# Scratch rows in (b, d) order: gathered embedding rows stored straight from the gather's tile

## The chip, the cores and the metric

The kernel runs on one core of one Trainium2 chip. The metric is the device time of one execution in microseconds (us). Before the change it is 2498.87 us, the median of three runs (2496.68 to 2500.59). All data are float32 unless said otherwise.

## What is computed

A recommendation tower. For each of B = 2048 samples, 39 ids pick one row of 16 floats from each of 39 tables; this is x0, of shape (B, 39, 16). Three layers of a compressed interaction network follow, then a small dense network on the sums and 16 dense features.

```python
e = stack([tbl_f[ids[:, f]] for f in range(39)], axis=1)      # (2048, 39, 16)
x0 = xk = e; direct = []
for idx, (W, b) in enumerate([(w0, b0), (w1, b1), (w2, b2)]): # W: (39, 39 or 64, 128)
    z = relu(einsum('bhd,bkd,hks->bsd', x0, xk, W) + b[None, :, None])
    if idx != 2: xk = z[:, :64]; direct.append(z[:, 64:])
    else: direct.append(z)
h = concatenate([sum(concatenate(direct, 1), -1), dense_ctx], 1)
h = relu(h @ W_top1 + b_top1); h = relu(h @ W_top2 + b_top2)
y = h @ W_top3
```

Every layer is a matmul over the products x0[h] * xk[k], with the pair (h, k) as the contracted index and (b, d) as the columns.

## The kernel before, in words

Samples are worked on in GROUPS = 16 groups of P = 128, and each group in CHUNKS = 4 chunks of CB = 32 samples, N = 32 x 16 = 512 columns. The order of the columns in a chunk is free as long as all tiles agree; before, it is (d, b).

GpSimd gathers: for each of the F = 39 fields an indirect DMA (L409) brings 128 rows of 64 B into `emb`, with the sample as the partition, 39 x 16 floats in each. The products need the field as the partition. So TensorE (PE) transposes `emb` in eight pieces of 78 columns into PSUM (`transpose_group`, L760 to L769; the two tiles of `turned` lie over `hi_copy`), ScalarE (ACT) copies them into `stage` (`fill_stage`, L588), and SP stores `stage` in a scratch tensor in HBM, `x0_transposed` (`xt`), 39 rows plus WRAP = 20 repeated ones, each COLS = 32768 floats long (`store_group`, L292). From there SP and ACT load, for every chunk, `x0_diag` (three bands of 39 partitions, seven tiles, for layer 0; `diag_band`, L254) and `x0_pairs` (64 partitions twice, 19 tiles, each row broadcast to 64 partitions, for layers 1 and 2; `pairs_half`, L262, and the last row to all 128, L331). `x0_pairs` has two buffers, `x0_diag` has one.

VectorE (DVE) multiplies into `prod`, a ring of four slots of four tiles (L479). Most tiles go to PE as float32 (L775, `plain_part`). For some, the product is split in a high part, made by ACT (L610), and a low part, made by DVE or GpSimd (L251, `low_part`), and PE multiplies three times (L796, `split_part`). In layer 2 all low parts are GpSimd's. PE takes the split tiles of layer 2 one slot behind the plain ones (`BEHIND`).

Every engine has a hand-written order, a loop over groups with four chunks in its body. In iteration c of group bt:

- PE: layer 1 of the chunk, layer 0 of the next chunk, layer 2 of the chunk. At c = 1, slot 1 of layer 2, it transposes group bt + 1 after it has waited for `gathered`.
- DVE: the products in the same order, the sums over d of z2 and of `direct01` (L530, L520).
- ACT: its half of the next chunk's pairs, the splits, the hand-ons of z, at c = 1 `fill_stage(bt + 1)`, its band of the chunk after next (L259 to L260).
- GpSimd: the low parts of layer 1 (`lows_of(1)`), ten gathers (`GATHERS_AT`: fields 20 to 29 and 30 to 38 of group bt + 1 at c = 0 and 1, fields 0 to 9 and 10 to 19 of group bt + 2 at c = 2 and 3), the low parts of layer 2 (`lows_of(2)`). At the end of c = 1 it waits for `gathered` and loads the next indices (L397). At c = 2, ahead of the gathers, `start_group` waits for the indices and for `turned_ready`, so that `emb` may be overwritten.
- SP: two bands of the next chunk once `summed2` allows it; at c = 2 then `store_group(bt + 1)`; then, once `prod_ready` shows the other buffer free, its pairs half. At c = 3 the chunk loaded is the first of group bt + 1, after a wait for `xt_stored`.

In the start, the same steps run one after the other: gather, transpose, copy, store, load bands, load pairs.

Of the kernel before, what the change touches and what calls it, by code (L numbers as in the profile page):

```python
# [29 lines left out]
ALU = mybir.AluOpType  # L30
# [7 lines left out]
CHUNKS = 4  # L38
CB = P // CHUNKS
# [54 lines left out]
PLAIN_TILES = {n: [t for t in range(TX - 1 if n else T0) if t not in SPLIT_TILES[n]] for n in SPLITS}  # L94
W_ORDER = (1, 2, 0)
W_SPLITS = {n: len(SPLIT_TILES[n]) + (n > 0) for n in SPLITS}
X0_DIAG_DMAS, X0_PAIRS_DMAS, ST_DMAS = 2 * DIAG, 3, 4
RAW_DMAS, WEIGHT_DMAS, TOP_DMAS = 2, 3, 10
H1, H2, DENSE = 512, 256, 16
DENSE_ROWS = 2 * 32 + DENSE  # L100
# [26 lines left out]
def build(nc, tables, ids, dense_t, w0f, w0s, w1, w2, small, wt1, wt1c, wt2, out):  # L127
# [5 lines left out]
    with ctx:  # L133
# [17 lines left out]
        logit2 = sb("logit2", [P, NB])  # L151
        idx = sb("idx", [P, F], I32)
        emb = sb("emb", [P, F * D])
        stage = sb("stage", [P, CHUNKS, D // 2, CB])
        ident = sb("ident", [P, P])
        w_plain = [sb(f"w{n}_plain", [P, len(PLAIN_TILES[n]), S]) for n in SPLITS]

        w_hi = [sb(f"w{n}_hi", [P, W_SPLITS[n], S], F32R) for n in SPLITS]
# [28 lines left out]


        hi_copy = ctx.enter_context(nc.psum_tensor("hi_copy", [P, 2, N], F32))
        turned = [hi_copy[:, 0, :], hi_copy[:, 1, :]]  # L190


        direct01 = ps("direct01")
# [10 lines left out]
        w_split = sem("w_split")  # L204
        weights_in = sem("weights_in")
        top_weights_in = sem("top_weights_in")
        ident_zero = sem("ident_zero")
        ident_ready = sem("ident_ready")
        first_idx_in = sem("first_idx_in")
        idx_in = sem("idx_in")  # L210
        waits_held = sem("waits_held")
        gathered = sem("gathered")
        turned_ready = sem("turned_ready")
        stage_ready = sem("stage_ready")
        xt_stored = sem("xt_stored")
        x0_diag_in = sem("x0_diag_in")
        x0_pairs_in = [sem(f"x0_pairs_in{i}") for i in range(2)]
# [54 lines left out]
        def _(sp):  # L272
# [19 lines left out]
            def store_group(bt):  # L292

                first = ahead(bt * (P * D))
                sp.wait_ge(stage_ready, 2 * (bt + 1))
                cols = xt[:, bass.ds(first, P * D)].rearrange(
                    "f (c e n) -> f c e n", c=CHUNKS, e=2)
                for half in range(2):
                    src = stage[half:2 * F:2].rearrange("p c d b -> p c (d b)")
                    sp.dma_start(cols[0:F, :, half, :], src).then_inc(xt_stored, 16)  # L300
                    sp.dma_start(cols[F:F + WRAP, :, half, :], src[0:WRAP]).then_inc(xt_stored, 16)

            def load_chunk(bt, c, store=False):

# [81 lines left out]

        @block.gpsimd
        def _(pool):
            nc.gpsimd.memset(ident[:], 0.0).then_inc(ident_zero, 1)
            pool.wait_ge(ident_zero, 1)  # L390
            nc.gpsimd.affine_select(out=ident[:], in_=ident[:], compare_op=ALU.not_equal, fill=1.0,
                                    base=0, pattern=[[-1, P]], channel_multiplier=1
                                    ).then_inc(ident_ready, 1)

            def load_indices(bt):

                pool.dma_start(idx[:], ids[bass.ds(bt * P, P), :]).then_inc(idx_in, 16)  # L397
# [1 line left out]
            def start_group(bt, first):  # L399
                if first:  # L400
                    pool.wait_ge(first_idx_in, 16)
                else:
                    pool.wait_ge(idx_in, 16 * bt)
                    pool.wait_ge(turned_ready, 2 * bt)
                    pool.sem_inc(waits_held, 1)

            def gather(fields):
# [50 lines left out]
        def _(dve):  # L458
# [56 lines left out]
            def sum01(bt, c):  # L515

                dve.wait_ge(direct01_ready, 2 * (bt * CHUNKS + c) + 2)
                if c == 0:
                    dve.wait_ge(window01_stored, 16 * (bt + 1))
                nc.vector.tensor_reduce(window01[:, c * CB:(c + 1) * CB],  # L520
                                        direct01[:].rearrange("p (d b) -> p b d", b=CB),
                                        AXIS.X, ALU.add).then_inc(summed01, 1)

            def sum2(bt, c):

                dve.wait_ge(direct2_ready, bt * CHUNKS + c + 1)
                if c == 1:
                    dve.wait_ge(window2_stored, 16 * (bt + 1))
                at = (c + CHUNKS - 1) % CHUNKS * CB
                nc.vector.tensor_reduce(window2[:, at:at + CB],  # L530
                                        z[2][:].rearrange("p (d b) -> p b d", b=CB),
                                        AXIS.X, ALU.add).then_inc(summed2, 1)

            dve.wait_ge(xk0_ready, 1)
# [50 lines left out]

        @block.scalar
        def _(act):
            def fill_stage(bt):  # L588
                if not (isinstance(bt, int) and bt == 0):
                    act.wait_ge(xt_stored, 16 * ST_DMAS * bt)  # L590
                for q in range(2):
                    act.wait_ge(turned_ready, 2 * bt + q + 1)
                    nc.scalar.copy(stage[0:2 * F, :, 4 * q:4 * q + 4, :].rearrange("p c d b -> p d c b"),
                                   turned[q][0:2 * F, :].rearrange("p (d c b) -> p d c b", d=4, c=CHUNKS)
                                   ).then_inc(stage_ready, 1)

            assert lows(2, V) <= 1

            def round_splits(n, some, slot, pos, used_by, chunk):
# [71 lines left out]
                nc.scalar.copy(w_hi[n][0:w_raw[n].shape[0]].rearrange("p t s -> p (t s)"), w_raw[n]  # L671
                               ).then_inc(w_hi_ready, 1)
            act.wait_ge(weights_in, 16 * WEIGHT_DMAS)
            fill_stage(0)
            act.wait_ge(xt_stored, 16 * ST_DMAS)
            act.wait_ge(w0_summed, 2)
            act.wait_ge(w_split, 3)
# [11 lines left out]
            def group(bt, last):  # L689
# [4 lines left out]
                for c in range(CHUNKS):  # L694
                    chunk = bt * CHUNKS + c
                    slot, pos = SL0 + chunk * SLC, SL0 + c * SLC
                    act.wait_ge(prod_ready, slot + 1)
                    if c < CHUNKS - 1:
                        load_second_half(bt, c + 1)
                    elif not last:  # L700
                        load_second_half(bt + 1, 0)
                    round_splits(1, slice(0, EARLY[1]), slot, pos, used_by, chunk)
                    direct_2(chunk, slot)
                    if not (last and c == CHUNKS - 1):
                        copy_xk0(chunk + 1)
                    round_splits(1, slice(EARLY[1], None), slot, pos, used_by, chunk)
                    slot, pos = slot + SLX, pos + SLX
                    if not (last and c == CHUNKS - 1):
                        round_splits(0, slice(0, None), slot, pos, used_by, chunk)

                        act.wait_ge(prod_ready, slot + SL0)
                    hand_on(1, xk2, b1_sb, slot)
                    nc.scalar.activation(direct01[0:HALF], z[1][HALF:P], ACT.Relu, bias=b1_sb[HALF:P]
                                         ).then_inc(direct01_ready, 1)
                    if c + 2 < CHUNKS:
                        load_last_band(bt, c + 2)
                    elif not last:
                        load_last_band(bt + 1, c + 2 - CHUNKS)
                    if last and c == CHUNKS - 1:
                        round_splits(2, slice(0, None), slot, pos, used_by, chunk)  # L720
                    else:
                        slot, pos = slot + SL0, pos + SL0
                        round_splits(2, slice(0, EARLY[2]), slot, pos, used_by, chunk)
                        hand_on(0, xk1, b0_sb, slot)
                        act.wait_ge(summed01, chunk + 2)
                        direct_0()
                        if c == 1 and not last:
                            fill_stage(bt + 1)

                            act.wait_ge(stage_ready, 2 * (bt + 2))  # L730
                        round_splits(2, slice(EARLY[2], None), slot, pos, used_by, chunk)

            with act.Fori(0, GROUPS - 1) as bt:
# [23 lines left out]

        @block.tensor
        def _(pe):
            def transpose_group(bt):  # L760
                pe.wait_ge(gathered, 16 * F * (bt + 1))
                if not (isinstance(bt, int) and bt == 0):
                    pe.wait_ge(stage_ready, 2 * bt)
                for d in range(D // 2):

                    ins = nc.tensor.transpose(turned[d // 4][0:2 * F, d % 4 * P:(d % 4 + 1) * P],  # L766
                                              emb[:, d:F * D:D // 2], ident[:])
                    if d % 4 == 3:
                        ins.then_inc(turned_ready, 1)  # L769

            def plain_part(n, t, i, held, first, last):

                rows = P if n else R0_LAST if t + i == T0 - 1 else R0
# [32 lines left out]
                        lows[s[3]] = lows[s[3]] + 1  # L806
                ins.then_inc(slot_free, 1)

            def layer(n, slot, pos, lows, turn=None, turn_at=None):

                last_slot = len(FIRST_TILE) - 1
                for k, t in enumerate(FIRST_TILE):
# [3 lines left out]
                    pe.wait_ge(prod_ready, slot + k + 1)  # L816
                    for i in plain:
                        plain_part(n, t, i, held, k == 0 and i == plain[0], False)
                    if k == turn_at:
                        transpose_group(turn)  # L820
                    if not BEHIND[n]:
                        split_parts(n, k, lows)
                    elif k > 0:
# [16 lines left out]
                    lows[s[3]] = lows[s[3]] + 1  # L840
                ins.then_inc(slot_free, SL0)

            pe.wait_ge(ident_ready, 1)
            transpose_group(0)
            pe.wait_ge(w0_summed, 2)
            pe.wait_ge(w_split, 3)
            pe.wait_ge(weights_in, 16 * WEIGHT_DMAS)
# [2 lines left out]
            def group(bt, last):  # L850
                for c in range(CHUNKS):
# [8 lines left out]
                        layer0(slot, pos, lows)  # L860
                        slot, pos = slot + SL0, pos + SL0
                    pe.wait_ge(summed2, chunk + 2)
                    if c == 1 and not last:
                        layer(2, slot, pos, lows, bt + 1, 1)
                    else:
                        layer(2, slot, pos, lows)

            with pe.Fori(0, GROUPS - 1) as bt:
                group(bt, False)
# [88 lines left out]
```

## Time and profile before

| | us |
|---|---|
| median of three runs | 2498.87 |
| the profiled execution | 2500.31 |
| its span | 2498.6 |
| PE busy | 2385.2 (95%) |
| VectorE busy | 2230.4 (89%) |
| GpSimd busy | 1709.7 (68%) |
| ScalarE busy | 1501.2 (60%) |
| bytes moved by DMA | 481.11 MB, mean 193 GB/s |

How to read it: the profile is one execution. Matmuls are pipelined and their ends are modelled, so a busy PE need not be at its peak. The granted clock is a share of full speed (1.00 is 2.4 GHz). DMA queue q1 is SP's, q10 is ScalarE's, q0 is GpSimd's. A DMA's packets on q1 and q10 are its contiguous rows, and one more on each engine for the count. "Idle before, releaser" tells how long an engine stood before an instruction and what ended that.

### The profile page before, as it was taken

The page shows a single profiled execution, that of the slowest core. Times are in us where ns is not written, and L with a number is a line of the kernel's source. Part 1 is how long each engine was busy: PE and PEld are TensorE (multiplying, and loading weights), DVE is VectorE, ACT ScalarE, POOL GpSimd, SP SyncE. Part 2 cuts the span into 40 slices and gives each one's busy share as a digit, 9 for nine tenths or more (in the row PEclk, how much of TensorE's full clock was granted, in tenths as well). Part 3 has the DMA queues.
Part 4 walks back from the last instruction along what each step waited for, and adds up shares of the span by engine and source line. Part 5 has one row for each costly group of instructions (what it writes and reads, how often), then busy time and mean ns, then how long its engine had stood idle before and what let it go on. Part 6 is the DMA issues. An engine that isn't in the chain of part 4 may idle for free.

```text
span 2498.6 us, 27181 instructions
## 1 busy us (share of the span) xinstructions
PE 2385.2 (95%) x7840; PEld 1468.9 (59%) x7840; DVE 2230.4 (89%) x1358; ACT 1501.2 (60%) x1798; POOL 1709.7 (68%) x1093
## 2 busy tenths in 40 slices
PE   0599999999999999999999999999999999999999
PEld 0266666666666666666666666666666666666653
DVE  0599999999999999999999999999999999999960
ACT  0366666666666666666666666666666666666652
POOL 6478777777777777677777777777776777754340
PEclk9899999999999999999999999999999999999999
DMA  2877877787777778777787877788787777867620
GB/s 69 237 207 190 222 210 199 190 214 209 190 210 209 208 182 217 208 197 199 213 216 178 215 211 202 190 215 218 181 211 212 206 182 213 222 183 202 199 62 0
DMA packets 267897, 481.11 MB, mean 193 GB/s; under 512 B 20075, under 2 KB 42715, under 8 KB 267797
## 3 DMA queue, kind: packets, MB, share of 16 engines
q1 hardware_dynamic: 146950, 275.14, 41.7%
q10 hardware_dynamic: 100480, 200.29, 28.9%
q0 software_dynamic: 20448, 5.45, 1.9%
q8 instruction: 9, 0.15, 0.0%
q14 instruction: 10, 0.08, 0.0%
HBM read 470.96 MB, written 9.84 MB: 192 GB/s over the span
## 4 chain that ended last, share of the span: by engine, by line
PE 70%; POOL 11%; issue 6%; DMA 6%; DVE 4%; ACT 2%; ACTq 0%; SPq 0%; POOLq 0%; DVEq 0%
PE z L796 34%; PE z L775 33%; POOL emb L409 7%; DMA emb<-in_tbl,idx 5%; DVE prod L479 4%; POOL lo_parts L251 4%; PE z L897 1%; DMA x_pairs<-x_transposed 1%; PE xk L897 1%; PE hi_copy L766 1%; ACT hi_parts L610 1%; PE direct L897 1%; DMA x_diag<-x_transposed 0%; ACT xk L630 0%; ACT xk L631 0%
## 5 line engine op out<-in xcount | busy, mean ns | idle before, releaser
L479 DVE TENSOR_TENSOR prod<-x_pairs,xk 128x2048 f32<-128x2048 f32 x640 | 1440.9, 2281 | 119.4 <-PE z L796 73.1
L775 PE MATMUL z<-prod,w_plain 128*128 128x512 f32 (+2 forms) x2688 | 1264.6, 595 | 40.2 <-DVE prod L479 40.2
L251 POOL TENSOR_TENSOR lo_parts<-prod,hi_parts 128x1024 fp32r<-128x1024 f32 x384 | 917.3, 2389 | 509.0 <-ACT hi_parts L610 486.0
L610 ACT CAST hi_parts<-prod 128x1024 fp32r<-128x1024 f32 x766 | 798.6, 1049 | 715.6 <-DVE prod L479 512.0
L796 PE MATMUL z<-hi_parts,w_lo 128*128 128x512 f32 (+1 forms) x1536 | 857.7, 558 | 1.1 <-DVE lo_parts L251 0.7
L409 POOL DMA_INDIRECT emb<-in_tbl,idx x624 | 701.9, 1125 | 196.0 <-issue 175.3
L775 PEld LDWEIGHTS z<-prod,w_plain 128*128 128x128 f32 (+2 forms) x2688 | 510.2, 190 | 440.1 <-issue 365.7
L796 PE MATMUL z<-hi_parts,w_hi 128*128 128x512 f32 (+1 forms) x1536 | 611.0, 398 | 0.0
L796 PE MATMUL z<-lo_parts,w_hi 128*128 128x512 f32 (+1 forms) x1536 | 606.7, 395 | 0.0
L796 PEld LDWEIGHTS z<-hi_parts,w_lo 128*128 128x128 f32 (+1 forms) x1536 | 289.9, 189 | 196.3 <-issue 145.0
L796 PEld LDWEIGHTS z<-lo_parts,w_hi 128*128 128x128 f32 (+1 forms) x1536 | 292.3, 190 | 189.5 <-issue 148.4
L796 PEld LDWEIGHTS z<-hi_parts,w_hi 128*128 128x128 f32 (+1 forms) x1536 | 288.5, 188 | 67.8
L251 DVE TENSOR_TENSOR lo_parts<-prod,hi_copy 128x1024 fp32r<-128x1024 f32 x256 | 310.2, 1212 | 2.9 <-ACT hi_copy L624 2.8
L479 DVE TENSOR_TENSOR prod<-x_diag,xk 117x2048 f32<-117x2048 f32 (+1 forms) x128 | 256.7, 2006 | 57.7 <-ACT xk L654 57.7
L624 ACT CAST hi_copy<-prod 128x1024 fp32r<-128x1024 f32 x256 | 259.1, 1012 | 2.1 <-DVE lo_parts L251 0.5
L630 ACT ACTIVATE xk<-z,columns 64x512 f32<-64x512 f32 x128 | 83.0, 648 | 145.3 <-PE z L796 143.7
L251 DVE TENSOR_TENSOR lo_parts<-prod,hi_parts 117x1024 fp32r<-117x1024 f32 x128 | 150.1, 1210 | 0.0
L245 POOL TENSOR_TENSOR half_parts<-prod,half_parts 64x512 fp32r<-64x512 f32 x64 | 81.9, 1280 | 5.5
L631 ACT ACTIVATE xk<-z,columns 64x512 f32<-64x512 f32 x128 | 83.5, 652 | 1.6
L766 PE MATMUL hi_copy<-ident,emb 128*78 128x128 f32 x128 | 18.3, 288 | 65.8 <-DMA emb<-in_tbl,idx 65.7
L606 ACT CAST half_parts<-prod 128x512 fp32r<-128x512 f32 x128 | 78.7, 615 | 0.0
L766 PEld LDWEIGHTS hi_copy<-ident,emb 128*78 128x78 f32 x128 | 14.3, 149 | 78.2 <-issue 78.1
(69 smaller groups left out, 652.0 us busy)
## 6 DMA issues: line engine op xcount, KB each, us to landing
x_pairs<-x_transposed SPq DMA_DIRECT2D x64, 2432.0 KB, 16.2
x_pairs<-x_transposed ACTq DMA_DIRECT2D x64, 2432.0 KB, 18.6
x_diag<-x_transposed SPq DMA_DIRECT2D x128, 546.0 KB
x_diag<-x_transposed ACTq DMA_DIRECT2D x64, 546.0 KB
x_pairs<-x_transposed SPq DMA_DIRECT2D x64, 256.0 KB, 19.6
emb<-in_tbl,idx POOLq DMA_INDIRECT x624
x_diag<-x_transposed SPq DMA_DIRECT2D x128, 78.0 KB
x_transposed<-stage SPq DMA_DIRECT2D x32, 156.0 KB
```

The lines of the kernel that those rows point to most:

```text
L245: engine.tensor_tensor(half_parts[0:HALF], held[0:HALF, at, :], hi, ALU.subtract).then_inc(done, 1)
L251: engine.tensor_tensor(lo_parts[0:rows, place:place + m, :], held[0:rows, at:at + m, :], hi, ALU.subtract).then_inc(done, 1)
L409: nc.gpsimd.indirect_dma_start(out=emb[:, f * D:(f + 1) * D], out_offset=None, in_=tables[f], in_offset=bass.IndirectOffsetOnAxis(ap=idx[: ...
L479: nc.vector.tensor_tensor(prod[0:rows, pos % RING, 0:n, :], a, xk.unsqueeze(1).broadcast_to([rows, n, N]), ALU.mult).then_inc(prod_ready, 1)
L606: nc.scalar.copy(half_parts[:], held[:, at, :]).then_inc(hi_ready, 1)
L610: nc.scalar.copy(hi_parts[0:rows, place:place + m, :], held[:, at:at + m, :]).then_inc(hi_ready, 1)
L624: nc.scalar.copy(hi_copy[:, 0:m, :].bitcast(F32R), held[:, at:at + m, :]).then_inc(hi_copied, 1)
L630: nc.scalar.activation(xk[0:HALF], z[layer][0:HALF], ACT.Relu, bias=b[0:HALF])
L631: nc.scalar.activation(xk[HALF:P], z[layer][0:HALF], ACT.Relu, bias=b[0:HALF]).then_inc(xk_ready[layer], 1)
L775: return nc.tensor.matmul(z[n][:], w, held[0:rows, i, :], start=first, stop=last)
L796: ins = nc.tensor.matmul(z[n][:], w, x, start=(first and i == 0), stop=(last and i == len(terms) - 1))
L897: ins = nc.tensor.matmul(acc[0:w.shape[1]], w, x, start=(k == 0), stop=(k == len(terms) - 1))
```

## The change

The scratch rows are laid out with the columns of a group in (b, d) order. SP waits for the gathers and stores `emb` as it is: for sample b and field f, 16 floats go to row f at column 16 b. Each group is stored by two DMAs in place of four. The transposes on PE, `turned`, `ident`, `stage`, ScalarE's two copies and the semaphores `turned_ready` and `stage_ready` are gone. GpSimd's `start_group` waits for `xt_stored`, since the store now reads `emb`. The two sums over d read (b, d) order. The loads of bands and pairs keep their shapes.

```diff
-X0_DIAG_DMAS, X0_PAIRS_DMAS, ST_DMAS = 2 * DIAG, 3, 4
+X0_DIAG_DMAS, X0_PAIRS_DMAS, ST_DMAS = 2 * DIAG, 3, 2
...
             def store_group(bt):
                 first = ahead(bt * (P * D))
-                sp.wait_ge(stage_ready, 2 * (bt + 1))
-                cols = xt[:, bass.ds(first, P * D)].rearrange(
-                    "f (c e n) -> f c e n", c=CHUNKS, e=2)
-                for half in range(2):
-                    src = stage[half:2 * F:2].rearrange("p c d b -> p c (d b)")
-                    sp.dma_start(cols[0:F, :, half, :], src).then_inc(xt_stored, 16)
-                    sp.dma_start(cols[F:F + WRAP, :, half, :], src[0:WRAP]).then_inc(xt_stored, 16)
+                sp.wait_ge(gathered, 16 * F * (bt + 1))
+                cols = xt[:, bass.ds(first, P * D)].rearrange("f (b d) -> b f d", d=D)
+                rows = emb[:].rearrange("p (f d) -> p f d", d=D)
+                sp.dma_start(cols[:, 0:F, :], rows).then_inc(xt_stored, 16)
+                sp.dma_start(cols[:, F:F + WRAP, :], rows[:, 0:WRAP, :]).then_inc(xt_stored, 16)
...
             def start_group(bt, first):
...
                     pool.wait_ge(idx_in, 16 * bt)
-                    pool.wait_ge(turned_ready, 2 * bt)
+                    pool.wait_ge(xt_stored, 16 * ST_DMAS * bt)
...
                 nc.vector.tensor_reduce(window01[:, c * CB:(c + 1) * CB],
-                                        direct01[:].rearrange("p (d b) -> p b d", b=CB),
+                                        direct01[:].rearrange("p (b d) -> p b d", d=D),
                                         AXIS.X, ALU.add).then_inc(summed01, 1)
...
-            def fill_stage(bt):
-                if not (isinstance(bt, int) and bt == 0):
-                    act.wait_ge(xt_stored, 16 * ST_DMAS * bt)
-                for q in range(2):
-                    act.wait_ge(turned_ready, 2 * bt + q + 1)
-                    nc.scalar.copy(stage[0:2 * F, :, 4 * q:4 * q + 4, :].rearrange("p c d b -> p d c b"),
-                                   turned[q][0:2 * F, :].rearrange("p (d c b) -> p d c b", d=4, c=CHUNKS)
-                                   ).then_inc(stage_ready, 1)
...
-                        if c == 1 and not last:
-                            fill_stage(bt + 1)
-
-                            act.wait_ge(stage_ready, 2 * (bt + 2))
...
-            def transpose_group(bt):
-                pe.wait_ge(gathered, 16 * F * (bt + 1))
-                if not (isinstance(bt, int) and bt == 0):
-                    pe.wait_ge(stage_ready, 2 * bt)
-                for d in range(D // 2):
-
-                    ins = nc.tensor.transpose(turned[d // 4][0:2 * F, d % 4 * P:(d % 4 + 1) * P],
-                                              emb[:, d:F * D:D // 2], ident[:])
-                    if d % 4 == 3:
-                        ins.then_inc(turned_ready, 1)
...
-                    if k == turn_at:
-                        transpose_group(turn)
```

## Rows read from the trace of the kernel before

**Rows 1.** The page: busy share of each engine, DMA by slice, queues.
```profile
PE 2385.2 (95%) x7840; PEld 1468.9 (59%) x7840; DVE 2230.4 (89%) x1358; ACT 1501.2 (60%) x1798; POOL 1709.7 (68%) x1093
...
DMA  2877877787777778777787877788787777867620
...
q10 hardware_dynamic: 100480, 200.29, 28.9%
```

**Rows 2.** Busy time by stretch: us, engines (instructions), granted clock, DMA share, GB/s.
```profile
1000.00:1153.00 153.00, 152.16 (x508) 95.00 (x507) 145.93 (x88) 98.09 (x118) 114.74 (x73) 1.00 0.77 199
1181.00:1189.00 8.00, 7.37 (x31) 5.22 (x32) 6.26 (x3) 6.22 (x9) 6.67 (x5) 1.00 0.28 73
1189.00:1197.00 8.00, 8.00 (x30) 5.18 (x29) 6.98 (x5) 5.28 (x6) 3.02 (x3) 1.00 0.93 208
1201.00:1205.00 4.00, 4.00 (x15) 2.46 (x13) 4.00 (x3) 3.02 (x5) 3.08 (x4) 1.00 1.07 337
```

**Rows 3.** GpSimd's index load in the loop: duration ns, first and last start us.
```profile
L397 POOL DMA_DIRECT2D idx<-in_ids x14: 577/580/587, 176.1 to 2061.5; - x14
```

**Rows 4.** ScalarE by time: start us, us, line, operation [idle before <-releaser].
```profile
1115.68 0.62 ACTq L265 DMA_DIRECT2D x_pairs<-x_transposed  x1
...
1151.46 0.63 ACTq L265 DMA_DIRECT2D x_pairs<-x_transposed  x1
...
1184.15 1.06 ACT L593 COPY stage<-hi_copy 78x512 f32<-78x512 f32 x2
...
1188.88 0.62 ACTq L265 DMA_DIRECT2D x_pairs<-x_transposed  x1
...
1210.93 0.33 ACTq L259 DMA_DIRECT2D x_diag<-x_transposed  x1
```

**Rows 5.** PE by time, layer 2 of chunks c = 1 and c = 2.
```profile
1181.63 1.09 PE L766 MATMUL hi_copy<-ident,emb 128*78 128x128 f32 x8 [1.06 <-DMA emb<-in_tbl,idx]
1182.47 0.48 PE L796 MATMUL z<-hi_parts,w_lo 128*128 128x512 f32 x1
...
1217.95 0.80 PE L796 MATMUL z<-hi_parts,w_lo 128*128 128x512 f32 x1
```

**Rows 6.** Packets of a queue at 30:50, 1.9:2.1 and 1107.8:1108 us; one issue.
```profile
DMA packets 512, 0.13 MB, mean 7 GB/s; under 512 B 256, under 2 KB 512, under 8 KB 512
q0 software_dynamic: 512, 0.13, 6.5%
...
q1 hardware_dynamic: 111, 0.02, 50.7%
...
q1 hardware_dynamic: 110, 0.05, 89.2%
...
1106.89 0.38 SPq L338 DMA_DIRECT2D sums<-logit  x1
sums<-logit SPq DMA_DIRECT2D x1, 64.0 KB, 2.1
```

**Rows 7.** SP's DMA issues by time, around the store of a group.
```profile
1173.03 0.32 SPq L259 DMA_DIRECT2D x_diag<-x_transposed  x1
...
1185.51 0.94 SPq L300 DMA_DIRECT2D x_transposed<-stage  x1
...
1189.72 0.70 SPq L265 DMA_DIRECT2D x_pairs<-x_transposed  x1
1190.60 3.81 SPq L331 DMA_DIRECT2D x_pairs<-x_transposed  x1
```

**Rows 8.** GpSimd by time: last gather of a group, next gathers, subtractions; the first subtraction.
```profile
1173.39 0.94 POOL L409 DMA_INDIRECT emb<-in_tbl,idx  x1 [0.30 <-issue]
...
1199.69 0.99 POOL L409 DMA_INDIRECT emb<-in_tbl,idx  x1 [0.44 <-issue]
...
1214.72 7.38 POOL L251 TENSOR_TENSOR lo_parts<-prod,hi_parts 128x1024 fp32r<-128x1024 f32 x3 [1.25 <-ACT hi_parts L610]
...
108.63 2.39 POOL L251 TENSOR_TENSOR lo_parts<-prod,hi_parts 128x1024 fp32r<-128x1024 f32 x1 [26.53 <-ACT hi_parts L610]
```

**Rows 9.** The chain that ended last, in the start: start us, us, what.
```profile
51.52 2.44 DMA emb<-in_tbl,idx
...
62.20 0.35 SPq L259
```

More of the change, by code:

```diff
@@ L153, in build @@
         emb = sb("emb", [P, F * D])
-        stage = sb("stage", [P, CHUNKS, D // 2, CB])
-        ident = sb("ident", [P, P])
         w_plain = [sb(f"w{n}_plain", [P, len(PLAIN_TILES[n]), S]) for n in SPLITS]
@@ L189, in build @@
         hi_copy = ctx.enter_context(nc.psum_tensor("hi_copy", [P, 2, N], F32))
-        turned = [hi_copy[:, 0, :], hi_copy[:, 1, :]]
         direct01 = ps("direct01")
@@ L206, in build @@
         top_weights_in = sem("top_weights_in")
-        ident_zero = sem("ident_zero")
-        ident_ready = sem("ident_ready")
         first_idx_in = sem("first_idx_in")
@@ L212, in build @@
         gathered = sem("gathered")
-        turned_ready = sem("turned_ready")
-        stage_ready = sem("stage_ready")
         xt_stored = sem("xt_stored")
@@ L388, in _ @@
         def _(pool):
[L389 to L393, printed above, removed]
             def load_indices(bt):
@@ L530, in sum2 @@
                 nc.vector.tensor_reduce(window2[:, at:at + CB],
-                                        z[2][:].rearrange("p (d b) -> p b d", b=CB),
+                                        z[2][:].rearrange("p (b d) -> p b d", d=D),
                                         AXIS.X, ALU.add).then_inc(summed2, 1)
@@ L673, in _ @@
             act.wait_ge(weights_in, 16 * WEIGHT_DMAS)
-            fill_stage(0)
             act.wait_ge(xt_stored, 16 * ST_DMAS)
@@ L807, in split_parts, with layer @@
                 ins.then_inc(slot_free, 1)
-            def layer(n, slot, pos, lows, turn=None, turn_at=None):
+            def layer(n, slot, pos, lows):
                 last_slot = len(FIRST_TILE) - 1
@@ L841, in layer0 @@
                 ins.then_inc(slot_free, SL0)
-            pe.wait_ge(ident_ready, 1)
-            transpose_group(0)
             pe.wait_ge(w0_summed, 2)
@@ L862, in group @@
                     pe.wait_ge(summed2, chunk + 2)
[L863 to L866, printed above, removed]
+                    layer(2, slot, pos, lows)
             with pe.Fori(0, GROUPS - 1) as bt:
```

## The prediction

> **What bounds the kernel now.** I read the busy shares first [rows 1]: TensorE (PE) is busy 95% of the span, VectorE 89%, GpSimd 68%, the 16 DMA engines 71 to 78% by slice. A share of 95% still hides a start without PE, so I looked at one stretch in the middle: of 153 us PE has 152.16 busy, at the full granted clock of 1.00 [rows 2]. In the steady part whatever stops PE moves the end one for one, and nothing gives it back. The period of a group (128 samples, four chunks) comes from the index load that GpSimd issues once a group: from 176.1 to 2061.5 us there are 13 periods, 145.03 us each [rows 3]. ScalarE's load of the second pairs half marks a fixed place in every chunk: 1115.68, 1151.46, 1188.88 [rows 4]. One ordinary chunk is 35.78 us, four of them 143.12, so a group has 1.91 us that three of its chunks do not have; the chunk that has them is c = 1, 37.42 us long. In PE's order of work it is visible: eight transposes begin at 1181.63 after 1.06 us of waiting for the last gathered rows, and the next split matmul stands at 1182.47, 0.84 us on [rows 5]. 1.06 + 0.84 = 1.90.
>
> **What goes.** The transposes and their wait: 15 in the loop (group 0's lie in the start), 15 x 1.91 = 28.6 us less, all of it on PE. ScalarE's two copies into `stage` (1.06 us at 1184.15 [rows 4]) lie beside PE's work and are worth nothing: ScalarE waits for products again right behind them. In the start they are on the path, counted below. The identity and its two instructions on GpSimd run before the indices have landed: nothing. The two sums on VectorE read PSUM with stride 1 instead of 32; at 0.68 us each with VectorE not setting the pace, I take nothing; if half of them fell away (128 x 0.34 us) PE would still set the pace.
>
> **What comes: the store.** Before, a group's 236 KB leave as runs of 1 KB: 4 DMAs, 39 x 4 x 2 + 20 x 4 x 2 = 472 rows. After, a run is one field of one sample, 16 floats = 64 B: 128 x 39 + 128 x 20 = 7552 rows, 472 on each of 16 engines where 30 were. The profile counts one packet for each row on SP's and ScalarE's queues, so I price the store by packet. No row shows 64 B written to HBM, so the price is bounded from both sides. From below: (a) GpSimd's gathers write 64 B rows packed eight to a packet: 6.5% of 16 engines in 20 us over 256 full packets is 81 ns a packet, 10 ns a row [rows 6]. (b) SP's load of the indices, 156 B rows: 111 packets in 0.2 us is 29 ns from packet to packet on an engine, of which 50.7%, 15 ns, busy [rows 6]. (c) SP's store of the sums, 512 B rows, 128 partitions, to HBM: 110 packets, 89.2% of 16 x 0.2 us, 26 ns each [rows 6]. (c) is the same queue, direction, memory and number of partitions, and (b) says that a row three times shorter isn't issued faster. I take 26 ns: 472 x 0.026 = 12.3 us a group. From above I take twice that, 52 ns (24.5 us), since a row far below 512 B might need its surroundings read before it is written.
> The page "DMA: Bandwidth & Descriptors" of the Trainium skill (Specifications) states that below 512 B the DMA engine does read-modify-write; no row of this trace shows such a write. By that rule the store would stand at the upper end, and the sum at the third rival's time.
>
> **Where the store lies.** Four DMAs at 0.8 to 0.9 us of SP's time become two. SP issues it behind the bands of the chunk (1173.0 to 1175.2) and ahead of the pairs (1189.72) [rows 7]. It waits now for `gathered`, whose last count comes at 1181.6 (that is what PE waited for [rows 5]): the last gather, begun at 1173.39 [rows 8], takes 8.2 us to land beside the bands against 2.44 us alone [rows 9]. First packet 0.9 us after the issue (sums store: issued 1106.89, packets from 1107.8 [rows 6]), so 1182.6. From 1187.0 (1188.88 less 1.9) ScalarE's half of the pairs asks for the same 16 engines, 64 x 19 rows of 2 KB, 76 per engine. A row of it costs 115 ns on average (28.9% of 16 x 2498.6 us over 100480 packets [rows 1]) and 147 ns in the stretch where both halves start (0.93 x 16 x 8 us over 208 GB/s x 8 us / 2048 B = 812 rows [rows 2]); 76 of them are 8.7 to 11.1 us, I take 10. If an engine takes one packet from each queue in turn, all 76 get in ahead of the store's end, since the store has 472. What bears this out is that gather, 5.8 us later in company. (The same page, Queues, rings and completion order, has the engines go round between queues by packets; the row agrees.) With 1.0 us from the last packet to the count (sums store: landed 2.1 us after the issue), the store has landed at 1182.6 + 12.3 + 10 + 1.0 = 1205.9.
>
> **Who waits for it.** `start_group` on GpSimd, at c = 2: before it waited for the transposes, long done; now the gathers of the group after next may not overwrite `emb` before the store has landed. Behind this wait are queued ten gathers (12.5 us with their gaps of 0.3) and then `lows_of(2)`, six subtractions that PE needs. Before: GpSimd reaches it at 1199.3, begins gathering at 1199.69, ends at 1213.5, idles 1.25 us, begins the first subtraction at 1214.72 [rows 8] and ends it at 1217.1; PE uses it at 1217.95 [rows 5]. Slack 1.25 + 0.85 = 2.1. In the new time, 1.9 earlier: 1199.3 + 2.1 - 1.9 = 1199.5 is the last moment without harm. So 1205.9 - 1199.5 = 6.4 us late; PE misses its low parts and stands. In general the loss is 0.472 t - 5.9 us for t ns per row. The loop has 14 such waits (the last two groups gather nothing; the one in the start is hidden, as the gathers for group 1 would end near 68 + 25 = 93 us and GpSimd's first subtraction, at 108.63, has 26.53 us of idle time ahead of it [rows 8]): 14 x 6.4 = 90 us.
> Others that wait: ScalarE's `load_last_band(bt+1, 0)` at 1210.93 [rows 4], 1209 in the new time, after 1205.9: nothing at 26 ns. SP's pairs stand behind the store in the same queue: 84 packets, some 12 us, landed near 1218, needed near 1224 + 6. Nothing, but this cover is gone at 40 ns, by when GpSimd's wait is longer anyway.
>
> **The start.** Gathers landed at 54.0, transposes, copies, four stores and landing, first band at 62.20 [rows 9]. After: 54.1 + 0.9 + 12.3 + 1.0 = 68.3, with no transposes to compete with: +6.1 us.
>
> **Sum.** -28.6 + 90 + 6.1 = +67.5 us on a span of 2498.6, 2566 us; the profiled execution took 2500.31, 1.7 more than its span, and 1.4 above the median 2498.87. So 2566 + 1.7 = 2568 us, 2.8% slower. This is the forecast, with 0.45.
>
> **Rivals.**
> First, the store hides (chance 0.22). If an engine overlaps a small packet of one queue with a large one of the other, or rows are packed as the gather's are, the 10 us drop out: landed at 1195.9, before 1199.5, loss zero up to t = 33 ns. For it: the 16 engines are only 28% busy from 1181 to 1189, and a share of 107% from 1201 to 1205 says that packets overlap [rows 2]. Against: late landings. Time: -28.6 + 6.1, 2478 us; with gather-priced rows (4.7 us) 2470. This is the other side from my forecast. It decides at a loss of 1.6 us per group, t = 16 with the full 10 us, or 37 without.
> Second, a partial hiding (0.05) between it and the forecast, about 1.5 us lost per group: 2499.
> Third, the short row costs double (0.23): 52 ns, loss 18.6 us x 14 = 261, start +18.4, -28.6: 2751 us. Then ScalarE also waits for it: landed at 1218, ScalarE at 1209, but it is the same delay and not added. For it: HBM writes of an eighth of the shortest write seen, 16 engines at once; each field's rows are 128 KB apart. Against: nothing but the steady 15 to 26 ns per short packet.
> Fourth, the edit moves the stall to ScalarE (0.05): if SP's 7552 rows block the unit that expands ScalarE's DMA too, ScalarE stands from 1187 until the store is nearly out, 1195; its next copy was due at 1188: 6 to 7 us for 15 groups, 90 to 105, about 2570. For it: SP's 3.81 us in one issue [rows 7].
> That the edit does nothing to PE isn't open: the transposes are gone from its queue.
>
> **Chances and range.** About 0.2% (5 us) is what a measurement here can tell from no change. Faster 0.23, same 0.05, slower 0.72. The range must take in the hidden case at its low end and the doubled price at its high end: 2465 to 2765. The likeliest case alone, t from 23 to 40 ns and 8.7 to 11.1 us of pairs, gives 2530 to 2670.
>
> **What would show it.** Right: a row "POOL emb <- DMA x_transposed<-emb" near 6 us x 14; PE idle before a split matmul of layer 2 at c = 2, waiting for GpSimd's low parts, nearly as large; chunk c = 1 down to 35.8 us, chunk c = 2 up to some 42; SP's queue with 113,000 more packets; the first band at 68 us. The first rival shows no such wait and 143.1 us a group. Wrong at the root: PE waiting for x_pairs or x_diag, which would say that DMA time as a whole, not the one wait, is the bound.

## The result and the profile after

The changed kernel takes 2468.41 us, median of four runs (2467.41 to 2470.75), against 2499.73 for the kernel before in the same runs: ratio 0.9876, 95% interval 0.9861 to 0.989. It is 31 us faster; I had forecast 2568 us, 68 us slower. What came is the first rival (2478 us, or 2470 with rows as cheap as the gather's): the store hides. One execution of the ten of an experiment below (the transposes back, with their wait) took 2771.23 us at a granted clock of 0.852 and stands in no comparison.

The page of the changed kernel: busy shares, DMA by slice, queues. They answer to [rows 1].

```profile
span 2465.7 us, 26690 instructions
...
PE 2366.6 (96%) x7712; PEld 1456.0 (59%) x7712; DVE 2229.2 (90%) x1358; ACT 1484.1 (60%) x1766; POOL 1706.1 (69%) x1091
...
DMA  2987878788787878878787887778778787877620
...
q1 hardware_dynamic: 260006, 275.13, 43.6%
```

SP's queue has 260006 packets, 113056 more than the 146950 before, as worked out (113280). The bytes are the same. All these rows cost the 16 engines 530 us of engine time together: 43.6% of 16 x 2465.7 less the 41.7% of 16 x 2498.6 of before. That would be 4.7 ns a row where I took 26; some of the difference of two large shares may be other rows' time, so the price is read from a clean stretch below.

One group in time. First GpSimd's index load, once a group (answers to [rows 3]); then ScalarE's issue of its pairs half in four chunks of one group and the next (answers to [rows 4]).

```profile
L382 POOL DMA_DIRECT2D idx<-in_ids x14: 574/579/582, 170.3 to 2031.9; - x14
```

```profile
1098.01 0.64 ACTq L258 DMA_DIRECT2D x_pairs<-x_transposed  x1
1133.79 0.63 ACTq L258 DMA_DIRECT2D x_pairs<-x_transposed  x1
1169.59 0.65 ACTq L258 DMA_DIRECT2D x_pairs<-x_transposed  x1
1205.39 0.63 ACTq L258 DMA_DIRECT2D x_pairs<-x_transposed  x1
1241.21 0.64 ACTq L258 DMA_DIRECT2D x_pairs<-x_transposed  x1
```

(2031.9 - 170.3) / 13 = 143.20 us a group, 1.83 less than 145.03. All chunks now have 35.8 us; the long one of 37.42 is gone. 15 x 1.83 = 27.5 us of the 31 to 33. The rest is in the start: VectorE's first product begins at 93.70 in place of 98.61, 4.9 us earlier.

The store by SP's issues, and GpSimd around its wait (answer to [rows 7] and [rows 8]).

```profile
1164.00 0.43 SPq L291 DMA_DIRECT2D x_transposed<-emb  x1
1164.71 3.15 SPq L292 DMA_DIRECT2D x_transposed<-emb  x1
1169.45 0.65 SPq L258 DMA_DIRECT2D x_pairs<-x_transposed  x1
```

```profile
1177.13 2.38 POOL L244 TENSOR_TENSOR lo_parts<-prod,hi_parts 128x1024 fp32r<-128x1024 f32 x1 [3.83 <-ACT hi_parts L586]
1180.08 0.98 POOL L394 DMA_INDIRECT emb<-in_tbl,idx  x1 [0.57 <-issue]
...
1194.90 7.38 POOL L244 TENSOR_TENSOR lo_parts<-prod,hi_parts 128x1024 fp32r<-128x1024 f32 x3 [1.19 <-ACT hi_parts L586]
```

Issued at 1164.0, 5.6 us ahead of ScalarE's pairs (I had 5.3), the store has its packets from 1165.0 to 1170.5 and has landed at 1171.7. SP's own pairs begin at 1170.5; ScalarE's first packet comes only at 1174.6, 5.0 us after its issue. GpSimd asks for the store at 1179.5. There is no wait: the 0.57 us before the gather at 1180.08 are issue. In the whole run GpSimd waits for the store once, 7.0 us, in the start, where nobody needs it.

SP's packets from 1166 to 1168 us (packets, MB, share of 16 engines):

```profile
DMA packets 2862, 0.18 MB, mean 92 GB/s; under 512 B 2862, under 2 KB 2862, under 8 KB 2862
...
q1 hardware_dynamic: 2862, 0.18, 89.3%
```

2862 rows in 2 us on 16 engines are 11.2 ns from row to row, 10 ns of it busy. 472 x 0.0112 = 5.3 us a group, not 12.3.

### The profile page after: what moved, and what is told of

Same layout as the page of the kernel before. It is cut to its first block, busy times and chain, and to the rows that moved or that the text cites. A ratio compares the mean times of both kernels' runs of the same rounds, so it can differ in the third digit from the quotient of the medians.

```text
span 2465.7 us, 26690 instructions
## 1 busy us (share of the span) xinstructions
PE 2366.6 (96%) x7712; PEld 1456.0 (59%) x7712; DVE 2229.2 (90%) x1358; ACT 1484.1 (60%) x1766; POOL 1706.1 (69%) x1091
## 3 DMA queue, kind: packets, MB, share of 16 engines
q1 hardware_dynamic: 260006, 275.13, 43.6%
## 4 chain that ended last, share of the span: by engine, by line
PE 95%; POOL 2%; DMA 2%; issue 1%; ACT 0%; DVE 0%; SPq 0%; ACTq 0%; POOLq 0%; DVEq 0%
PE z L735 46%; PE z L756 46%; POOL emb L394 1%; PE z L850 1%; PE xk L850 1%; DMA x_pairs<-x_transposed 1%; PE direct L850 1%; DMA x_diag<-x_transposed 0%; POOL lo_parts L244 0%; DVE prod L464 0%; DMA x_transposed<-emb 0%; ACT x_pairs L723 0%; DMA emb<-in_tbl,idx 0%; ACT hi_parts L586 0%; DMA idx<-in_ids 0%
## 5 line engine op out<-in xcount | busy, mean ns | idle before, releaser
L630 ACT COPY xk<-x_diag 117x512 f32<-117x512 f32 x64 | 37.3, 582 | 58.2 <-DMA x_diag<-x_transposed 58.2
L756 PE MATMUL z<-half_parts,w_lo 128*128 128x512 f32 x128 | 51.2, 400 | 0.0
```

Source lines behind the costliest of these rows:

```text
L756: ins = nc.tensor.matmul(z[n][:], w, x, start=(first and i == 0), stop=(last and i == len(terms) - 1))
```

## The experiments

The first four ran on one chip, the second four on another, on which the kernel before took 2511.29 us instead of 2498.9. Times of the second four are set against that one, and group periods against the unchanged loop of the last of them.

**The changed kernel again.**

> The changed kernel once more, beside the others of this call, as their measure. Theory (the gain is the eight transposes and their wait, 15 times, plus a shorter start): 2468 us, 1.83 us less per group than before (period of a group 143.2 us against 145.0), first product of VectorE near 94 us. What is open is the start: the first load of the pairs took 20.5 us in the changed kernel and 24.6 us before. If that belongs to the kernel it is 20 to 21 us again; if it is a matter of the single execution it differs.

2469.21 us (before: 2498.9; ratio 0.9882, 0.9865 to 0.9898). The first load of the pairs took 19.73 us from the issue on the chain that ended last, near the 20.5 of the first trace. Those are two executions of the changed kernel against one of the kernel before.

**The transposes back, with their wait.**

```diff
+                pe.wait_ge(gathered, 16 * F * (bt + 1))
+                for d in range(D // 2):
+                    ins = nc.tensor.transpose(hi_copy[0:2 * F, d // 4, d % 4 * P:(d % 4 + 1) * P],
+                                              emb[:, d:F * D:D // 2], ident[:])
+                ins.then_inc(turned_ready, 1)
```

> The changed kernel with the eight transposes of emb put back on PE at their old place, with the wait for the gathers, their result unused (no copies by ScalarE, the direct store stays). Theory (all of the loop's gain was PE's time): 15 x 1.9 us = 28 us more than the changed kernel, 2496 us, and a group's period of 145.0 us again. Rival (part of the gain came from ScalarE's copies, from stride-1 sums or from another order of the transfers): less than 20 us more, under 2488 us.

2496.84 us, 27.6 us above the changed kernel of the same call. The group has its old period, from GpSimd's index loads less the first:

```profile
L392 POOLq MOVE idx<-in_ids x14: 29/29/38, 167.0 to 2052.8; - x14
```

(2052.8 - 167.0) / 13 = 145.06. The chunks are 37.27, 36.33, 35.82 and 35.78 us by ScalarE's pairs. ScalarE's copies, the four stores in place of two, and the sums' stride of the kernel before are not put back here, so they were worth nothing that can be seen: the whole gain of the loop is PE's queue.

**The transposes back, without the wait.** The same, but they read a tile that nothing writes in the loop.

> As the one before, but the transposes read a tile that is never written in the loop, so PE doesn't wait for the gathers. Theory: only the transposes' own 0.84 us remain, 15 x 0.84 = 12.6 us more than the changed kernel, 2481 us. If the wait costs nothing by itself (PE would have stood there anyway): the same 2496 us as with the wait.

2474.24 us, only 5.0 above, not 12.6.

```profile
L394 POOLq MOVE idx<-in_ids x14: 29/29/38, 169.4 to 2035.7; - x14
```

143.56 us a group, 0.36 more. This does not mean that the transposes cost only 0.36 us. PE never stands in the middle of either kernel, and it runs at the full granted clock. First the changed kernel, then this one, from 400 to 2200 us (us, PE busy and its instructions, PEld, VectorE, ScalarE, GpSimd, granted clock, DMA share, GB/s):

```profile
400.00:2200.00 1800.00, 1800.00 (x5933) 1120.78 (x5932) 1743.89 (x1058) 1142.85 (x1356) 1336.04 (x845) 1.00 0.79 206
400.00:2200.00 1800.00, 1800.00 (x6022) 1125.38 (x6022) 1740.88 (x1056) 1142.47 (x1353) 1335.51 (x845) 1.00 0.79 206
```

Yet this one does more in the time. PE's block of eight plain matmuls, once a chunk, comes every 35.80 us in the changed kernel; here (start us, us, what; the transposes lie between the last two rows):

```profile
840.48 3.44 PE z L755 x8
876.14 3.44 PE z L755 x8
912.69 3.44 PE z L755 x8
```

35.66 us for a chunk without transposes, 36.55 for one with them. The transposes cost 0.89 us where they stand, 15 x 0.89 = 13.4 us, near the 12.6 expected. And every chunk, with or without them, is 0.14 us shorter than in the changed kernel, 64 x 0.14 = 9.0 us. Together that is 4.4 us more, 5.0 were measured. The shorter chunks are no time that PE took back from a wait, as there is none: its matmuls follow each other a little faster. In the kernel before, in the changed one and in the transposes with their wait a chunk is 35.80. This kernel has one more tile in SBUF (`fixed`, 2.5 KB a partition) than the kernel with the wait; whether that is the cause, no run here tells. So 2474.24 us can't be read as the price of the transposes, nor the 22.6 us up to 2496.84 as that of the wait. By PE's rows the kernel with both has, in the group at 1176 us, 1.01 us of waiting and 0.85 of transposes, together the 1.86 by which its group is longer.

**The first group stored in two parts.**

```diff
+            sp.wait_ge(first_gathered, 16 * WRAP)
+            sp.dma_start(cols[:, F:F + WRAP, :], rows[:, 0:WRAP, :]).then_inc(xt_stored, 16)
+            sp.dma_start(cols[:, 0:WRAP, :], rows[:, 0:WRAP, :]).then_inc(first_stored, 16)
+            sp.wait_ge(gathered, 16 * (F - WRAP))
+            sp.dma_start(cols[:, WRAP:F, :], rows[:, WRAP:F, :]).then_inc(xt_stored, 16)
```

> The changed kernel, with group 0 stored in two parts: fields 0 to 19 (with their repeated rows) as soon as they are gathered, fields 20 to 38 at the end. Everything else as in the changed kernel. Theory (rows cost near 11 ns each on an engine, 472 of them 5.5 us; now 152 stand behind the last gather, 1.8 us): the first band 3.5 us earlier, 2465 us. Rival (the landing is mostly fixed latency, or the pairs' load takes back what is gained): under 1.5 us, 2467 us or more.

2467.31 us (ratio to before 0.987, 0.9854 to 0.9887), 1.9 us less than the changed kernel beside it; their intervals overlap, so this isn't shown as a gain. Its chain in the start, and that of the changed kernel of the same call (start us, us, what):

```profile
54.30 3.34 DMA x_transposed<-emb
58.99 10.07 DMA x_diag<-x_transposed
69.86 23.70 DMA x_pairs<-x_transposed
93.77 2.30 DVE prod L476
```

```profile
54.92 6.64 DMA x_transposed<-emb
62.92 9.56 DMA x_diag<-x_transposed
73.27 19.73 DMA x_pairs<-x_transposed
93.22 2.30 DVE prod L464
```

The store lands in 3.34 us in place of 6.64, as expected, and the load of the pairs takes all of it back, 23.70 against 19.73. Both of my lines were half right: the price was, and so was the taking back.

**Store twice, store thrice.** The store itself made longer, at its place.

```diff
-                cols = xt[:, bass.ds(first, P * D)].rearrange("f (b d) -> b f d", d=D)
+                for to in (xt, *extra):
+                    cols = to[:, bass.ds(first, P * D)].rearrange("f (b d) -> b f d", d=D)
```

> The changed kernel with each group stored twice, the second time to a scratch tensor that nothing reads; all waits for the store wait for both. 944 rows of 64 B per engine, 11 ns each: 11 us, so now the store is still under way when ScalarE's half of the pairs starts. Theory A (an engine takes packets in turn, the store is held up by the 76 rows of 2 KB, 9 to 11 us): landed some 5 us after GpSimd's last harmless moment, 14 x 4 to 5 us, with 5.5 us in the start: near 2534 us. Theory B (small and large packets overlap, nothing is added): landed before GpSimd asks, 5.5 us in the start only: 2474 us.

> As the one before, with each group stored three times: 1416 rows per engine, 16.4 us. Theory A (in turn): landed near 10.7 us too late, 14 times, and 11 us in the start: 2630 us. Theory B (overlap): landed 0.7 us too late, 2489 us. In both GpSimd shows a wait for the store at c = 2; if the time rises without such a wait, the DMA time as a whole is the bound.

2610.89 us (ratio 1.04, 1.0382 to 1.0417) and 2680.08 us (1.0672, 1.0654 to 1.069). It is the mechanism of theory A, but its times were 2534 and 2630 us, too low by 77 and 50; 13 us of each are the slower chip. Twice, in the trace, GpSimd around the wait; and the packets of SP (q1) and ScalarE (q10) in 1090 to 1094, 1094 to 1098 and 1102 to 1106 us:

```profile
1099.11 2.36 POOL L246 TENSOR_TENSOR lo_parts<-prod,hi_parts 128x1024 fp32r<-128x1024 f32 x1 [3.85 <-ACT hi_parts L589]
1110.61 2.64 POOL L397 DMA_INDIRECT emb<-in_tbl,idx  x1 [9.14 <-DMA extra<-emb]
...
1126.90 0.80 PE L759 MATMUL z<-hi_parts,w_lo 128*128 128x512 f32 x1 [6.25 <-POOL lo_parts L246]
```

```profile
q1 hardware_dynamic: 5138, 0.33, 79.2%
q10 hardware_dynamic: 29, 0.06, 4.6%
...
q10 hardware_dynamic: 455, 0.93, 96.3%
q1 hardware_dynamic: 456, 0.03, 12.3%
...
q10 hardware_dynamic: 344, 0.67, 76.8%
q1 hardware_dynamic: 2078, 0.13, 42.9%
```

Alone, SP's rows pass at 5138 in 4 us. As soon as ScalarE's rows of 2 KB are there, the queues have 455 and 456: in turn, 140 ns for one of each, and the short rows crawl until the long ones are through. The counts keep together in stretches as short as 0.14 us, 10 to 23 of each and never more than 4 apart. The first issue was at 1086.11, GpSimd goes on at 1110.61: 24.5 us for 944 rows. GpSimd stands 9.14 us, PE 6.25 us for the low parts that are late. A group takes 152.74 us against 144.23 in the unchanged loop on that chip (the last kernel below), 8.5 more. All of it lies where PE stands, and standing is not all of it. PE has nothing to do from 1120.7 on; here is what was granted to it while it stood, and when it went on at 1126.90:

```profile
1123.00:1126.80 3.80, 0.00 (x0) 0.00 (x0) 0.00 (x0) 1.18 (x2) 3.48 (x3) 0.51 0.89 211
1126.90:1129.60 2.70, 2.70 (x6) 2.15 (x7) 0.00 (x0) 0.00 (x0) 2.60 (x2) 0.50 0.87 150
```

The granted clock fell to its lower level, 1.2 GHz, while PE stood, and PE's matmuls, which start 0.235 us apart otherwise, started 0.43 us apart until about 1129.7. From group to group this adds 1.6 to 3.0 us to the 6.3 to 6.4 us of standing, on average 2.3 (the third group and those after it). Three times: 157.1 us a group, 12.9 more, of which 10.4 are standing and the rest again the lower clock; GpSimd waits 225.6 us in all for the last copy. The waits of 0.8 to 1.1 us in the kernel before do not lower the clock; it is 1.00 from 400 to 2200 us.

**The store behind the pairs.**

```diff
-                if store:
-                    store_group(bt + 1)
...
                              ).then_inc(x0_pairs_in[c % 2], 16)
+                if store:
+                    store_group(bt + 1)
```

> The changed kernel with SP issuing the store of the next group behind its pairs of the chunk instead of ahead of them, nothing else. The rows wait in SP's queue for 84 large rows per engine. Theory (the place hides the store, and GpSimd's wait is on the path once it is late): landed near 25 us after the pairs' issue, 13 us too late, 14 times: near 2650 us. Rival (GpSimd's wait is taken up by its idle time, or ScalarE's wait comes first): under 2500 us, or more than 2650 with ScalarE named as the one that waits.

2685.81 us (ratio 1.0691, 1.0673 to 1.0709). Who waited for whom (us in total, times, longest):

```profile
POOL emb L394 <- DMA x_transposed<-emb: 236.8, 15, 17.7
...
PEld z L756 <- POOL lo_parts L244: 225.1, 133, 14.2
PE z L756 <- POOL lo_parts L244: 173.3, 31, 13.3
```

On its chip the changed kernel would take 0.988 x 2511.3 = 2481 us; a group takes 14.4 us more than the unchanged one there (158.66 against 144.23), and 14 x 14.4 = 202 us are the difference to within 3 us; I had expected 13 us of lateness. PE stands for 12.0 of the 14.4 us on average, and the other 2.4 go by the granted clock of 0.50 behind each stall. Nothing but the place in SP's order has changed, and the kernel goes from 1.2% faster to 6.9% slower. ScalarE, the other that waits for the store, is not named among the large waits.

**Rows by size, and two queues at once.** A tail behind the output: `probe_store(n)` stores 39 x 128 rows of n floats. ScalarE issues the load after the seventh store, and once more when it has landed, beside SP's last two stores.

```diff
+            for n in (16, 8, 16, 32, 64, 128, 256):
+                probe_store(n)
+                done += 1
+                sp.wait_ge(probe_stored, 16 * done)
+            sp.wait_ge(probe_loaded, 16)
+            for i in range(2):
+                probe_store(16, i * P * 16)
```

> The changed kernel with a tail behind the output's store: SP stores 39 x 128 rows from SBUF to HBM, 312 per engine, one DMA after the other has landed, with rows of 64, 32, 64, 128, 256, 512 and 1024 B; then ScalarE loads 64 x 19 rows of 2 KB alone, then the same load beside two stores of 64 B rows (624 per engine). Its time is longer by this tail and isn't compared. Theory (an engine's price per row has a floor near 11 ns, set by the number of rows): 64 B and 32 B both land in 5 us, 512 B in 9.6 us (26 ns), 1 KB in 14 us (40 ns). Rival (the short price is owed to the bytes, or 64 B suffers below 512 B): 32 B lands in half the time of 64 B, or costs more. For the two queues: in turn by packets, the stores land at 16 to 18 us, instead of 8.7 alone; overlapping, within 2 us of 8.7 us.

SP's packets in the middle of the stores of 64 B (2483 to 2484 us), 32 B (2488 to 2489), 128 B (2498 to 2499), 256 B (2504 to 2506) and 512 B (2511 to 2515), then 1 KB (2525 to 2530); last, 2556 to 2560, the 64 B stores beside ScalarE's load:

```profile
q1 hardware_dynamic: 1701, 0.11, 87.7%
...
q1 hardware_dynamic: 1700, 0.05, 75.0%
...
q1 hardware_dynamic: 1654, 0.21, 142.8%
...
q1 hardware_dynamic: 1699, 0.43, 95.6%
...
q1 hardware_dynamic: 2268, 1.16, 101.0%
...
q1 hardware_dynamic: 1698, 1.74, 103.9%
...
q10 hardware_dynamic: 407, 0.83, 97.9%
q1 hardware_dynamic: 408, 0.03, 13.4%
```

| row | from row to row on one engine |
|---|---|
| 32 B | 9.4 ns |
| 64 B | 9.4 ns |
| 128 B | 9.7 ns |
| 256 B | 18.8 ns |
| 512 B | 28.2 ns |
| 1 KB | 47 ns |

(16 engines x stretch / packets.) 32, 64 and 128 B land in 5.1 us each, 312 rows an engine, as expected. From 256 B on the price rises by 18.8 ns for each further 512 B; for 1 KB I had expected 40 ns. The two 64 B stores beside the load landed after 19.8 us where 624 rows at 9.4 ns are 5.9 us, near the 16 to 18 of taking turns: the first rival's overlap is refuted for such rows.

## Why the prediction was wrong, point by point

**What goes: right.** 15 x 1.91 = 28.6 us was forecast; 27.5 is the difference of the two traces, and 27.6 came back with the transposes and their wait. That all of it lies on PE holds too. The division, 0.84 us of transposes and 1.06 of waiting for the gathers, is the one that PE's rows show again when both are put back (0.85 and 1.01). The 1.06 was one group's; the wait differs by some tenths from group to group, so the term came out 1.1 us too large.

**The price of a row: this step failed.** "I take 26 ns" came from the sums' store with 512 B rows, row (c) of [rows 6], and for 512 B it is right (28.2 ns by the tail). The step from there to 64 B rested on row (b): 111 packets in 0.2 us, 29 ns each, "says that a row three times shorter isn't issued faster". That reading was wrong. The stretch of 0.2 us held one small DMA with eight rows an engine and was only 50.7% busy; it showed how a short DMA comes up, not how fast a long one goes. The 15 ns busy in the same row were nearer, and row (a), 10 ns, the nearest: I had called it the bound from below and set it aside. Measured: 11.2 ns in the kernel, 9.4 ns alone. The term of 12.3 us is 5.3. The third rival, 52 ns, did not come either: nothing doubles below 512 B; the time of a row falls with the bytes down to 128 B and is level below.
The page "DMA: Bandwidth & Descriptors" of the Trainium skill (Specifications) has the engines do read-modify-write below 512 B. No run here shows whether they do. If they do, a row does not get dearer by it: 28.2 ns at 512 B, 9.4 at 64 B.

**Contention: right in kind, and not met.** The 10 us for ScalarE's 76 rows are 10.7 us by the store made twice (140 ns x 76), and the turns are exact. The page "DMA: Bandwidth & Descriptors" of the Trainium skill (Queues, rings and completion order) says that engines go round between queues by packets; 455 against 456 agrees. But the store of the changed kernel is out of the engines at 1170.5, and ScalarE's rows come at 1174.6: they do not meet. A store of 12.3 us, from 1165.0 to 1177.3, would have met them. I had added the 10 us whatever the store's length, "since the store has 472", and did not ask whether the store would be over first. At 11 ns my formula with the 10 us still gives 0.472 x 11.2 - 5.9, below zero, so by its own point of decision (16 ns) the sum flips on the price alone.

**Who waits: the mechanism was right.** Made late by length or by place, the store holds GpSimd, GpSimd's low parts hold PE, 14 times; the row that I named shows up, with 142 to 237 us. The store made twice lands about as late as I had thought the single one would: 23.7 us after its first issue (1086.11 to 1109.8), where I had 24.3 (1181.6 to 1205.9). PE then stood for 6.3 to 6.4 us, and I had 6.4. What my sum lacks is the clock. It took a stall to cost its own length, "one for one", but behind each of these stalls PE went on at a granted clock of 0.50, and 8.5 us were lost per group. Had the price of a row held, these 2.1 us more in each of 14 groups would have made some 2597 us of my 2568; this is an estimate.

**The start: wrong sign.** +6.1 us was forecast, -4.9 came. Store and landing take 7.2 us (53.89 to 61.06) in place of 8.1 (54.10 to 62.20): with 5.3 for 12.3 that term is as expected. The other 4 us lie in the load of the pairs, 20.5 us against 24.6 before, which I had not touched. It is 18.8 to 21.7 us in the seven experiments that keep group 0's store in one piece, and 23.7 where it was split. In its first 6 us SP's queue and ScalarE's move, in the kernel before:

```profile
q10 hardware_dynamic: 457, 0.94, 59.4%
q1 hardware_dynamic: 131, 0.27, 17.1%
```

and in the changed one:

```profile
q10 hardware_dynamic: 417, 0.85, 44.4%
q1 hardware_dynamic: 316, 0.65, 35.2%
```

In the kernel before, SP's half comes into its stride late (131 rows, 141 with group 0 in two parts), and ScalarE's doesn't use the time. But the second trace of the same changed kernel has 452 rows of SP and 224 of ScalarE, so the share differs between executions too. Over the ten traces, where one of the queues has fewer than 150 rows in its first 6 us the load takes 21.3 to 24.6 us, and where both have more than 220 it takes 18.8 to 21.0. Why one begins late, no run here tells; that stays open. It is 4 us by the two traces; by the medians of the two calls, 31.3 and 29.7 us in all, less 27.5 for the loop and 0.9 for the store, it is 1 to 3 us. No term of my forecast had it.

**The rivals.** The first had the right sign, on the grounds of overlap (refuted: exact turns) or of rows priced as the gather's (right in size, 10 ns against 11.2, though they are not packed: 113056 more packets). With that price it said 2470 us. That this is within 2 us is partly luck: the loop gave 1.1 us less than its term, and the load of the pairs at the start gave what no term had. The fourth, a stall of ScalarE, does not appear: its pairs go out at 1169.59, 0.65 us long. The range, 2465 to 2765, held the time of 2468.41 near its lower edge; the sign that I gave 0.72 to did not hold.

## What to carry to other kernels

Price a DMA of many short rows from a stretch in which the engines are full. A DMA of a few rows per engine shows only how it starts: 29 ns from row to row at 50.7% busy, where full engines needed 9.4 to 11.2. Two queues on the same engines go in turn, row by row: here a DMA of many short rows was cheap while alone and slowed more than tenfold while the other queue had long rows, so ask first whether it is over before they come, and where it stands in the order. When work leaves the bounding engine, look at the wait in front of it as well as at its own time; here the wait was the larger half. When you price a stall, look at the granted clock behind it. And when you take a piece of work away or put it back, check that the rest keeps its pace: the kernel with one more tile ran every chunk 0.14 us faster, 9 us in all.

## What the runs showed of the hardware that I had not expected

- Rows stored from SBUF to HBM cost 9.4 ns on an engine at 32 and at 64 B and 9.7 at 128 B, then 18.8, 28.2 and 47 ns at 256, 512 and 1024 B.
- With 64 B rows on one queue and 2 KB rows on the other, each had the same number of packets, 407 and 408 in 4 us; a turn took 157 ns, where a 64 B row alone took 9.4.
- SP's instruction for 2560 short rows behind 4992 others took 3.15 us, and 13.99 us in the store made twice, while ScalarE's rows went in between; SP's next issues stood that long.
- In stalls of PE of 6.3 to 13.3 us the granted clock fell to 0.50, and PE went on at 0.50 behind them, which cost 1.6 to 3.1 us more each time; stalls of up to 1.1 us left the clock at 1.00.
- With `fixed` in SBUF and eight transposes a group, a chunk without transposes took 35.66 us of PE in place of 35.80, both at a granted clock of 1.00 and without idle time.
- ScalarE's load of the pairs had its first packet 4.2 to 5.0 us after its issue in the changed kernel.
